# Full-array products of constants ahead of the first score jobs of a two-lane decoder kernel

## The reference

```python
x = x + _L0_attn_ref(_layernorm(x, axis=-1), Wq, Wk, Wv, rel_bias_table, ln_gamma, ln_beta)
# in _L0_attn_ref:
attn = softmax(einsum('bhqd,bhkd->bhqk', q, k) * scale) + rel_bias
out = einsum('bhqk,bhkd->bhqd', attn, v)
out = layernorm(out) * ln_gamma + ln_beta
```

## Time and profile before

| | us |
|---|---|
| median of 3 runs (lowest, highest) | 584.02 (583.33, 591.06) |
| the profiled execution, its time | 586.47 |
| the profiled execution, span from first to last instruction | 584.7 |
| mean granted TensorE clock over the span | 0.954 of full speed |

### The profile page before, as it was taken

How to read it: one execution, slowest core, us unless ns; L and a number is a source line. 1 busy time by engine, 2 the same in 40 slices (tenths; PEclk the granted TensorE clock), 3 DMA queues, 4 the chain that set the end, 5 groups by cost and what they waited for, 6 DMA issues and landing times.

```text
span 584.7 us, 13038 instructions
## 1 busy us (share of the span) xinstructions
PE 515.5 (88%) x4832; PEld 321.4 (55%) x4842; DVE 425.0 (73%) x1232; ACT 331.8 (57%) x825; POOL 199.0 (34%) x309
## 2 busy tenths in 40 slices
PE   3887888999999999977488997998989989999995
PEld 2532444544455576756344556776667867655543
DVE  7878567254666667588998768753788557798996
ACT  1764435755768879655267573566566644353441
POOL 6940000024365545341345520000224221434774
PEclk9955889999999999999699999999998989999998
DMA  8700000000300000001324833000000000301101
GB/s 291 307 1 4 2 3 4 2 1 0 145 2 1 1 2 3 2 1 34 169 84 135 179 86 101 3 4 2 2 3 3 3 2 2 145 0 67 80 1 36
DMA packets 25889, 27.93 MB, mean 48 GB/s; under 512 B 18249, under 2 KB 22866, under 8 KB 24930
## 3 DMA queue, kind: packets, MB, share of 16 engines
q1 hardware_dynamic: 25826, 27.10, 14.4%
HBM read 22.14 MB, written 4.75 MB: 46 GB/s over the span
## 4 chain that ended last, share of the span: by engine, by line
PE 59%; DVE 19%; issue 8%; ACT 5%; SPq 3%; DMA 2%; POOL 2%; POOLq 0%; DVEq 0%; ACTq 0%
PE B_banks L312 4%; PE A_banks L312 4%; PE A_banks L2108 2%; PE A_banks L248 2%; PE A_banks L1014 2%; PE A_banks L1027 2%; DVE B_moe_h L2075 2%; SPq L276 2%; PE B_banks L248 2%; PE A_banks L1874 1%; DVE A_l0a_nmax L340 1%; PE B_banks L982 1%; PE A_banks L1884 1%; PE B_banks L1035 1%; PE A_banks L1035 1%
## 5 line engine op out<-in xcount | busy, mean ns | idle before, releaser
L2108 PE MATMUL A_banks<-A_moe_xT,w_moe_rows 128*128 128x512 f32 x72 | 36.0, 617 | 1.3 <-DVE A_moe_h L2075 1.3
L832 POOL TENSOR_TENSOR A_l0x_prob<-A_l0x_prob,A_l0x_inverted_sums 128x256 f32<-128x256 f32 (+1 forms) x32 | 25.9, 831 | 28.5 <-DVE A_l0x_inverted_sums L947 28.5
L2108 PE MATMUL B_banks<-B_moe_xT,w_moe_rows 128*128 128x512 f32 x72 | 34.4, 598 | 1.2 <-DVE B_moe_h L2075 1.1
L832 POOL TENSOR_TENSOR B_l0x_prob<-B_l0x_prob,B_l0x_inverted_sums 128x256 f32<-128x256 f32 (+1 forms) x32 | 25.9, 831 | 27.6 <-DVE B_l0x_inverted_sums L947 27.6
L160 POOL TENSOR_TENSOR A_l0a_rstd<-A_l0a_ve,w_const_rows 128x4 f32<-128x4 f32 x2 | 2.0, 1016 | 87.8 <-DVE A_l0a_ve L156 87.8
L379 ACT ACTIVATE A_l0a_expT<-A_banks 128x512 f32<-128x512 f32 x32 | 18.3, 603 | 18.6 <-PE A_banks L327 18.3
L849 ACT ACTIVATE B_l0x_prob<-B_l0x_prob,B_l0x_nmax 128x128 f32<-128x128 f32 x64 | 28.2, 446 | 0.9 <-DVE B_l0x_nmax L929 0.9
L849 ACT ACTIVATE A_l0x_prob<-A_l0x_prob,A_l0x_nmax 128x128 f32<-128x128 f32 x64 | 28.2, 447 | 0.0
L340 DVE TENSOR_REDUCE A_l0a_nmax<-A_banks 128x2 f32<-128x512 f32 x32 | 21.7, 687 | 8.0 <-PE A_banks L248 7.7
L379 ACT ACTIVATE B_l0a_expT<-B_banks 128x512 f32<-128x512 f32 x32 | 18.4, 600 | 15.9 <-PE B_banks L327 15.9
L340 DVE TENSOR_REDUCE B_l0a_nmax<-B_banks 128x2 f32<-128x512 f32 x32 | 21.9, 688 | 7.3 <-PE B_banks L248 7.3
(11 more groups left out here) (602 smaller groups left out, 1598.6 us busy)
## 6 DMA issues: line engine op xcount, KB each, us to landing
w_toeplitz_rows<-in_toeplitz_rows SPq DMA_DIRECT2D x1, 3072.0 KB, 13.1
w_moe_rows<-in_moe_rows SPq DMA_DIRECT2D x1, 2304.0 KB, 8.6
w_l1x_rows<-in_l1x_rows SPq DMA_DIRECT2D x1, 2048.0 KB, 8.4
A_l1x_values<-A_l1a_v_tokens SPq DMA_DIRECT2D x4, 512.0 KB, 2.6
A_l1x_v_groups<-A_l1x_values SPq DMA_DIRECT2D x16, 128.0 KB, 3.3
B_l1x_values<-B_l1a_v_tokens SPq DMA_DIRECT2D x4, 512.0 KB, 3.4
B_l1x_v_groups<-B_l1x_values SPq DMA_DIRECT2D x16, 128.0 KB, 3.3
w_l0x_vo_rows<-in_l0x_vo_rows SPq DMA_DIRECT2D x1, 1024.0 KB, 13.7
```

The source lines that it names most:

```text
L832: ins = pool.tensor_tensor(pair, pair, bcast(rz[:, g % 2, i, :], 2, n), ALU.mult)
L2108: pe.matmul(hidden_bank(k)[:, :], w["moe_w3" if which else "moe_w1"][:, ORDER[i], part, :], xT[:], start=True, stop=True).then_inc(s_h.sem, 1)
```

## The change

`tensor_S` takes an optional pair of operands, `fill`. Where it is given, one product is issued behind the job's waits and ahead of its own products: stationary the bf16 identity (128 x 128), moving a bf16 constant of 128 x 512 (`other_token`, which `rel_attention` doesn't use otherwise), into the job's whole bank. It carries no semaphore. The job's own first product starts the bank anew, so what the added product left is replaced. Each lane gives it for jobs 0 to 15: 12 ahead of the loop and 4 in it, so 32 products (and 32 loads of stationary operands) are added in the kernel. Both constants are made by the weight program's conversion, for which TensorE already waits in `project(0)`. No wait, transfer or order is changed.

```diff
--- before.py
+++ after.py
@@ -233,7 +233,7 @@
     def exp_bank(self, u):
         return self.bank[1 + u % 2]
 
-    def tensor_S(self, pe, m):
+    def tensor_S(self, pe, m, fill=None):
         b, c, h, n = self.job(m)
         bank = self.score_bank(m)
         if m == self.JOBS or m >= self.first:
@@ -243,6 +243,8 @@
         if self.shifted is not None and bank is self.bank[0]:
             pe.wait_ge(*self.s_shT(self.shifted + 1))
             self.shifted = None
+        if fill is not None:
+            pe.matmul(bank[:, :], *fill, start=True, stop=True)
         if c is None:
             for c in range(SB):
                 ins = pe.matmul(bank[:, c * S:(c + 1) * S], self.q(b, h, c * P, P), self.k(b, h, 0, S),
@@ -643,6 +645,9 @@
         dve.tensor_tensor(x[:], y[:], xb, ALU.add).then_inc(s_x.sem, 1)
 
     def tensor(pe):
+
+        steady = (w["ident_bf"][:], w["other_token"][:].rearrange("p a b -> p (a b)"))
+        FILLS = U // 2
         yield 4.5
         w.loaded(pe, "const")
         tensor_transpose_tiles(pe, w, bank[0], xn, s_xn, s_xTp)
@@ -696,7 +701,7 @@
             if u == a.JOBS:
                 a.tensor_shift(pe, 0)
                 yield SCORES + 1.2 * u + 0.8
-            a.tensor_S(pe, u)
+            a.tensor_S(pe, u, steady if u < FILLS else None)
             if 4 * SB + u < STEPS:
                 yield
                 transpose_stack(4 * SB + u)
```

## The result

| | before | after |
|---|---|---|
| median (lowest to highest), 20 runs each | 583.94 (577.5 to 591.06) | 587.33 (582.42 to 590.05) |
| ratio, 95% interval | | 1.0078 (1.0052 to 1.0103) |
| the profiled execution, its time, span | 586.47, 584.7 | 585.72, 583.9 |
| granted clock of the profiled execution | 0.954 | 0.973 |

What follows compares the result with a forecast made beforehand. TensorE was taken as the bound at half clock from 32.0 to 41.0 us, then a chain with DVE. Clock gains of -8.7, products +5.3, and +0.3 and +0.3 for crowding and series gave -2.8: 581.2 us, range 577 to 590.

Steps and rivals of the forecast that it cites:

- The clock until the first sum over keys: The clock stays full from 32 us to past the first sum over keys, gaining 8.7 us before the products' cost.
- Rivals 1 and 2: Clock falls anyway at 32 us, 595.3 us, chance 0.12; or in the gap at 41 to 42, 590 us, chance 0.12.
- Part (a): 33.26 to 40.83 us, transposes and B's score jobs at full clock: 3.0 us gained, 0.4 more from two groups ahead.
- the pair's 0.3: A's job 7 and B's job 0, side by side before, run in series at 32.65 us: 0.3 us lost.
- Part (b): 42.11 to 57.70 us, TensorE's pieces in the chain with DVE at full clock: 3.1 us gained.
- Part (c): First sum over keys from 3.57 to 1.86 us, with shift, exponents and job behind it: 2.2 us gained.
- The products' price: 24 of 32 added products lie on the chain at 0.22 us: 5.3 us, plus 0.3 and 0.3 for crowding and series.
- rival 3: Each added product costs 0.33 us because the job's load can't be drawn ahead; 583.8 us, no change; chance 0.12.
- the -2.8: The forecast change of the whole time in us, to 581.2 us; chance 0.50.
- What the engine did before the clock moved: Around 32.0 us: the clock fell after the f32 projections ended and only transposes and 64-row score jobs followed.
- Rival 4: The clock also stays up from 79.7 to 83.2 us: 1.5 us more gained, 579 down to 577 us; chance 0.14.
- The range: The whole time lies between 577 and 590 us, likeliest 581.2.

Runs made afterwards that it cites:

- fills_20: The changed kernel with the added product ahead of each lane's jobs 0 to 19 instead of 0 to 15; median 589.7 us, ratio to before 1.0123.
- late_8_15: The changed kernel with the added product only ahead of each lane's jobs 8 to 15; mean 590.0 us, median 592.1, runs from 578 to 597.
- ahead_12_17: The changed kernel, but for jobs 12 to 17 the product goes to bank 3, ahead of the job's wait; median 585.9 us, ratio to before 1.0018.
- double: The changed kernel with two added products instead of one ahead of each of jobs 0 to 15; median 591.5 us, ratio to before 1.0140.
- rows_64: The changed kernel with the added product on the job's own 64 rows (its queries stationary), still 512 columns; median 586.9 us, ratio to before 1.0066.
- before_again: The kernel before, unchanged, run for a second trace; median 582.5 us, ratio to before 0.9990.
- before_3: The kernel before, unchanged, run for a third trace; 581.57 us.
- before_4: The kernel before, unchanged, run for a fourth trace; 584.52 us.
- ahead_only: The changed kernel with products only for jobs 12 to 17, into bank 3 ahead of the wait; median 588.2 us, ratio to before 1.0098.

## Why the prediction was wrong

**The clock until the first sum over keys: right in direction, short at the end.** Full from 20.1 to 57.7 us where the first trace had half from 32.0. Rivals 1 and 2 are out in this trace: no fall at 32 or in the gap at 41 to 42. But it fell 2.2 us ahead of the sum over keys, and not for want of added products: B's jobs 13 and 14 had theirs at 55.32 and 56.82, only A's job 16 (57.59) had none, and in fills_20, where it has one, the clock fell still earlier in the work. Between 50.45 and 57.6 us TensorE was busy for 5.16 of 7.15 us, in jobs with waits between them; that this is why it fell isn't shown, since late_8_15 kept the clock through the same instructions.

**Part (a), 3.4 us gained: the step that failed.** It took one execution's half-clock stretch from 32 to 41 us for the kernel's. In the three other traces of the kernel before, and in three more of the same code, the clock is full there and DVE's maxima are the bound. Against the first trace the change is 0.55 us shorter in this part (12.61 to 12.06), about what the sum gives for it (3.4 less eleven products at 0.22 and the pair's 0.3: 0.7); against the usual 9.62 it is 2.44 us longer, because 0.33 + 0.22 + 0.32 = 0.87 on TensorE takes the place of DVE's 0.62, ten times. The numbers that could have warned were in the prediction itself: at full clock TensorE's repetition is 0.33 + 0.32 = 0.65, below the 0.69 that it gives for DVE, so without the products DVE is the bound as soon as the clock is full.

**Part (b), 3.1 us gained.** The products ate more than that: the second part is 11.73, against 11.15 in the first trace and 10.45 in the others.

**Part (c), 2.2 us gained: absent.** The sum over keys is 3.57 in both. Where the clock does hold (late_8_15, ahead_12_17) it is worth what was forecast: 10.6 to 10.8 against 12.7 to 13.1, some 2.2 us.

**The products' price, 5.9 us with the jobs in series: 7.5 measured** as excess. The 0.22 holds behind transposes. Where the product stands alone rival 3's 0.33 is right. A second product on the same operands costs 0.21 (double), and what comes on top is the step between 128 and 64 rows; whether the engine spends it on a load that can't be drawn ahead, as rival 3 has it, no row shows. From A's job 12 to the end of job 13, with B's 9 and 10 between, TensorE needs 2.6 us (47.86 to 50.45) for 2.23 by my sum (three at 0.54 and a lone 0.61): all four products take 0.32. The first three jobs cost 0.33 + 2 x 0.22 instead of 3 x 0.22.

**The sum.** From the usual trace before: +0.8 ahead of the first DVE anchor, +2.4, +1.3 and +0.5 in the three parts, +5.0 us in the stage. Against the first trace it is +0.8, -0.55, +0.6 and +0.3, +1.1 us: also for the execution from which it was reckoned the -2.8 had the wrong sign. So of the 7.8 us between -2.8 and +5.0, half (3.9) is the choice of trace, 2.2 is part (c), and most of the rest the dearer products that stand alone or between jobs. The mean moved by 3.1. The kernel has 15.4 us less at half clock (35.7 against 51.1), which at 0.285 gives back 4.4 of the excess of 7.5. Of these 15.4 about 10 are in the stage (6.8 against 17.1 us); the others are dips later on, and no run here separates their causes.

The Trainium skill's page "TensorE: Matmul & The Clock Gate", section "Part 3: Packing small matmuls", stood behind rival 3: loads overlap products in flight only where their row groups differ. A load that isn't hidden would fit the step between 128 rows and 64, where 0.10 us shows; products on the same rows show none: 0.43 for two of 512 columns (double), and 0.22 for a 64-row job behind a product of its own rows (rows_64). The same section of the Trainium skill also lets a load into the background weight buffer go ahead of products in flight, and no row here says which loads are of that kind.

**What the engine did before the clock moved.** I read the fall at 32 us as following from transposes and 64-row jobs without projections. In before_again the last projection ends at 27.7 us, and through 13 us of little else than the same two kinds of work, 10.34 us busy, the clock stays full until 40.8. The Trainium skill's page "TensorE: Matmul & The Clock Gate", section "Part 4: PE-mode transpose", says transposes don't count as busy in the same way. The first trace seemed to agree; in before_again, before_3 and before_4 the same alternation, half of it transposes, kept the full clock, so it isn't shown as the cause of the fall at 32. What parts the first execution from these is open.

**Rival 4**, a gain at 79.7 to 83.2 us: the dip is still there, at 81.6 to 85.0. **The range** held the time, and by luck, since the -2.8 us beneath it had the wrong sign; its likeliest part, 579 to 585, rested on one execution, while the three runs given with it already spread over 7.7 us (583.33 to 591.06).

## What to carry to other kernels

Work added to hold the clock is paid in every execution and earns only in those in which the clock would have fallen, so read several traces of the kernel as it is before you count a half-clock stretch as its own, and ask of each stretch which engine is next once TensorE is at full clock. Price an added product by what stands on both sides of it, not by its columns alone, and put it into time that the engine spends waiting; at half clock that time is gone.

## What the runs showed of the hardware

Where the clock fell in this stage differed by 9 us between executions of the same program (32.0, and 40.8 to 41.0 three times), and with the fall at 32.0 the stage was 3.9 us longer than the mean of the other three. The whole time differs by more than 12 us between executions and rises with the us at half clock (0.285 us for each, 73 runs); the three traces with the usual stage still have 577.95, 581.57 and 584.52 us, and differ behind it. Changing between operands of 128 rows and of 64 rows costs TensorE about 0.10 us at full clock: transposes and jobs 0.33 and 0.32 in alternation, 0.22 where one follows its like, and the same with the added product of either kind.
The clock stayed down for 20.5 us in ahead_only with TensorE busy for nearly all of it, among them whole-array products of 512 columns, and rose behind the first sum over keys; with two such products for each job it rose at 47.8.
